# A transformer tower on one core: the keys' bias times the queries, taken from eight more columns of the queries' product

## What is computed

```python
# token reduction: each 4x4 patch (16 pixels) becomes one token of 64 channels, 256 tokens an image
q  = LN(mean over patch) @ Wq.T;  k, v = LN(pixels) @ Wkv.T          # 8 heads of 8
h  = mean + (softmax(q*scale . k over the 16 pixels) . v) @ proj_w.T + proj_b
# causal linear attention with decay over the 256 tokens of an image, chunks of 128
h  = layernorm(h + lightning_attn(h @ w_qkv) @ w_proj + b_proj)
# mixture of experts: 8 experts of 64x64, the best two per token
h  = layernorm(h + moe(h))
```

## Time and profile before

| | |
|---|---|
| Time, median of 3 | 2586.48 us (2584.95 to 2589.83) |
| The profiled execution's own time | 2589.41 us |
| Its span | 2587.0 us |
| PE, DVE, ACT, POOL busy | 87%, 79%, 72%, 71% |
| Mean granted clock of TensorE | 0.985 |

### The profile page before, as it was taken

The page is one execution under the profiler, slowest core; times in us unless marked ns, Lnnn a source line. Parts: engine busy times, 40 slices in busy tenths (PEclk is TensorE's granted clock), DMA queues, the critical chain, the costliest instruction groups (busy, mean ns, idle before and its releaser), DMA issues. The chain is left out here.

```text
span 2587.0 us, 91002 instructions
## 1 busy us (share of the span) xinstructions
PE 2248.5 (87%) x32685; PEld 1057.8 (41%) x32685; DVE 2053.0 (79%) x3996; ACT 1851.1 (72%) x4405; POOL 1839.2 (71%) x1949
## 2 busy tenths in 40 slices
PE   1888898888888888888888888888888885999997
PEld 1344444444444444444444444444444442222222
DVE  4588888887888888888888888888888886777775
ACT  2877777777777777777777777777777773555554
POOL 3688788887888888888888888888888862233333
PEclk9999999999999999999999999999999996999999
DMA  4433333333333333333333333333333300010001
GB/s 79 83 67 67 66 66 66 67 66 57 64 67 67 67 67 67 67 67 67 67 67 67 67 67 67 67 67 67 67 67 67 67 2 1 17 23 22 20 20 29
DMA packets 573783, 147.92 MB, mean 57 GB/s; under 512 B 573504, under 2 KB 573504, under 8 KB 573504
## 3 DMA queue, kind: packets, MB, share of 16 engines
q1 hardware_dynamic: 573504, 143.53, 29.0%
HBM read 135.10 MB, written 8.39 MB: 55 GB/s over the span
## 5 line engine op out<-in xcount | busy, mean ns | idle before, releaser
L709 POOL TENSOR_TENSOR pv<-vs,aw 128x512 f32<-128x512 f32 x512 | 540.2, 1086 | 306.5 <-DVE aw L912 306.5
L856 DVE TENSOR_TENSOR kqs<-ps,qqT 128x512 f32<-128x512 f32 x512 | 354.1, 692 | 299.5 <-PE ps L393 295.2
L595 ACT ACTIVATE xd<-xb 128x512 f32<-128x512 f32 x512 | 585.4, 1178 | 0.0
L388 PE MATMUL ps<-xb,w_ckv 64*64 64x512 f32 x2048 | 555.6, 619 | 5.0 <-DVE kqs L856 5.0
L393 PE MATMUL ps<-xb,w_ckv 64*64 64x512 f32 x2048 | 555.6, 619 | 0.0
L577 ACT ACTIVATE sqs<-ps 128x512 f32<-128x512 f32 x512 | 308.4, 602 | 247.2 <-PE ps L393 246.9
L753 POOL TENSOR_TENSOR xt<-xb 128x512 f32<-128x512 f32 x256 | 325.8, 1273 | 23.0 <-issue 22.6
L716 POOL TENSOR_TENSOR pv<-pv 128x512 f32<-128x512 f32 x256 | 320.5, 1271 | 0.0
L867 DVE TENSOR_TENSOR sm<-ps,decay 128x1024 f32<-128x1024 f32 x256 | 299.5, 1208 | 4.4 <-PE ps L471 4.4
L415 PE MATMUL ps<-w_ckv,xd 64*64 64x64 f32 x16384 | 301.1, 223 | 0.0
L415 PEld LDWEIGHTS ps<-w_ckv,xd 64*64 64x64 f32 x16384 | 266.1, 136 | 33.1 <-issue 3.0
(11 more groups left out here) (223 smaller groups left out, 4261.6 us busy)
## 6 DMA issues: line engine op xcount, KB each, us to landing
xb<-in_x_dram SPq DMA_DIRECT2D x512, 256.0 KB, 4.4
out_dram<-outb SPq DMA_DIRECT2D x128, 64.0 KB, 1.6
w1p<-in_L_ffn_w_dram SPq DMA_DIRECT2D x16, 16.0 KB
w2p<-in_L_ffn_w_dram SPq DMA_DIRECT2D x8, 16.0 KB
b1p<-in_L_ffn_b_dram SPq DMA_DIRECT2D x8, 0.2 KB
b2v<-in_L_ffn_b_dram SPq DMA_DIRECT2D x8, 2.0 KB
sm<-in_L_tok_Wkv_dram SPq DMA_DIRECT2D x4, 16.0 KB, 2.0
w_av<-in_L_attn_w_qkv_dram SPq DMA_DIRECT2D x4, 16.0 KB, 2.1
```

What stands on the lines that cost most here:

```text
L388: nc.tensor.matmul(KB[own, :], w_ckv[own, 2 * P + m * C:2 * P + (m + 1) * C], xv[own, j], start=True, stop=True)
L595: nc.scalar.activation(xd[:, j, :].rearrange("p (b t) -> p b t", b=ST), xb[:, f, :].rearrange("p (b t d) -> p d b t", b=ST, d=ST)[:, j], A ...
L709: nc.gpsimd.tensor_tensor(pv[:, at].rearrange("p (k d) -> p k d", d=D), vs[:, s, at].rearrange("p (k d) -> p k d", d=D), aw[:, j * W4:(j + ...
L856: V.tensor_tensor(kqs[:, j, :].rearrange("p (t d) -> p t d", d=ST), KB.rearrange("p (t d) -> p t d", d=ST), qqT[:, s, :].unsqueeze(2).to_b ...
```

## The change

The bias matmul L369 goes, and the last transpose signals tr_pe. w_qc gets eight more columns, the queries' weights times the keys' bias by head, so L430 writes 136 columns per image. Two DVE instructions behind L891 multiply the eight columns with the root and add cb_row, the keys' bias times the queries' bias, into sbq, a buffer of four slots in SBUF; the softmax reads it two steps later. mx and mxb move from SBUF to columns 25 and 26 in PSUM. The setup gets two small matmuls and four DVE instructions.

```diff
--- before.py
+++ after.py
@@ -111,7 +111,8 @@
         selk = sb("selk", [P, TG])
         selv = sb("selv", [P, TG])
         selbk = sb("selbk", [P, SL])
-        w_qc = sb("w_qc", [P, P])
+        w_qc = sb("w_qc", [P, P + HEADS])
+        cb_row = sb("cb_row", [P, SL])
         w_pj = sb("w_pj", [P, P])
         w_aq = sb("w_aq", [P, P])
         w_av = sb("w_av", [P, 2 * C + CR])
@@ -169,10 +170,9 @@
             y0s = sb1("y0s", [P, N, 3])
             yrs = sb1("yrs", [P, N, 3])
             eps_c = sb1("eps_c", [P, 1])
-            mxb = sb1("mxb", [P, SL])
             sb2 = sb1("sb2", [P, SL])
             aw = sb1("aw", [P, N * SL])
-            mx = sb1("mx", [P, SL])
+            sbq = sb1("sbq", [P, 4, SL])
             den = sb1("den", [P, SL])
             rden = sb1("rden", [P, SL])
             agg = sb1("agg", [P, P])
@@ -329,6 +329,8 @@
                 pe.wait_ge(s_dve0, 1)
                 for j in range(4):
                     nc.tensor.transpose(ps[:, 0, j * P:(j + 1) * P], cat[:, j, :], ident[:])
+                nc.tensor.matmul(ps[:, 5, 0:SL], cat[:, 0, :], selbk[:], start=True, stop=True)
+                nc.tensor.matmul(ps[:, 5, SL:2 * SL], scr[:, 0, :], selbk[:], start=True, stop=True)
                 for j in range(2):
                     nc.tensor.transpose(ps[:, 2, j * P:(j + 1) * P], kqs[:, 0, j * P:(j + 1) * P], ident[:])
                 pe.wait_ge(s_act0, 1)
@@ -365,9 +367,8 @@
                             pe.wait_ge(den_done, done(i, r, 2, 1))
                             sv = ssb[:].rearrange("p (t d) -> p d t", d=ST)
                             for d in range(ST):
-                                nc.tensor.transpose(SB[:, d * P:(d + 1) * P], sv[:, d, :], ident[:])
-                            nc.tensor.matmul(sgr[:, :, 25:26], qqT[:, o, :], selbk[:], start=True,
-                                             stop=True).then_inc(tr_pe, 1)
+                                mm = nc.tensor.transpose(SB[:, d * P:(d + 1) * P], sv[:, d, :], ident[:])
+                            mm.then_inc(tr_pe, 1)
 
                     def keys_free(j):
 
@@ -427,7 +428,7 @@
                                 pe.wait_ge(st_ev, pairs(i, r, 0, 2))
                             for m in range(2):
                                 own = slice(m * C, (m + 1) * C)
-                                mm = nc.tensor.matmul(B67[:, m, 0:P], h1[own, 4 * i + r + 1, 0:P], w_qc[own, :],
+                                mm = nc.tensor.matmul(B67[:, m, 0:P + HEADS], h1[own, 4 * i + r + 1, 0:P], w_qc[own, :],
                                                       start=True, stop=True)
                             mm.then_inc(qp_pe, 1)
 
@@ -805,6 +806,7 @@
                     for m in range(2):
                         link(V.tensor_copy(cat[:, j, m * C:(m + 1) * C], rows[:, j, :]))
                 link(V.tensor_copy(bq_c[:], col[:, 0:1]))
+                link(V.tensor_copy(scr[:, 0, :], col[:, 0:1].to_broadcast([P, P])))
                 link(V.tensor_scalar(selbk[:], headmask[:], col[:, 1:2], WS, ALU.mult, ALU.mult))
                 link(V.scalar_tensor_tensor(w_ckv[:, 0:P], blockmask[:], -1.0 / C, ident[:], ALU.mult, ALU.add))
                 for m in range(2):
@@ -824,8 +826,11 @@
                 for m in range(2):
                     h = slice(m * C, (m + 1) * C)
                     link(V.tensor_scalar(w_qc[h, 0:C], ps[h, 0, m * C:(m + 1) * C], 1.0 / N, None, ALU.mult))
+                    link(V.tensor_scalar(w_qc[h, P:P + HEADS], ps[h, 5, m * HEADS:(m + 1) * HEADS], 1.0 / N, None,
+                                         ALU.mult))
                 for j, dst in ((1, w_ckv[:, 2 * P:3 * P]), (2, w_ckv[:, P:2 * P]), (3, w_pj[:])):
                     link(V.tensor_tensor(dst, ps[:, 0, j * P:(j + 1) * P], blockmask[:], ALU.mult))
+                link(V.tensor_copy(cb_row[:], ps[:, 5, SL:2 * SL]))
                 link(V.tensor_scalar(w_ckv[:, P:3 * P], w_ckv[:, P:3 * P], WS, None, ALU.mult))
                 link(V.tensor_copy(qdec[:], ps[:, 1, 2 * P:3 * P]))
                 link(V.tensor_copy(kqs[:, 1, 0:2 * P], ps[:, 2, 0:2 * P]))
@@ -889,19 +894,25 @@
                     if there(i, r, -1):
                         dve.wait_ge(tq_pe, done(i, r, 0, 1))
                         V.tensor_tensor(heads(q2[:]), B67[:, :, 0:C], yrs[:, 2:4, 2:3].to_broadcast([P, 2, C]),
-                                        ALU.mult).then_inc(q2_done, 1)
+                                        ALU.mult)
+                        for m in range(2):
+                            ins = V.scalar_tensor_tensor(sbq[:, (r + 1) % 4, m * HEADS:(m + 1) * HEADS],
+                                                         B67[:, m, P:P + HEADS], yrs[:, 2 + m, 2:3],
+                                                         cb_row[:, m * HEADS:(m + 1) * HEADS], ALU.mult, ALU.add)
+                        ins.then_inc(q2_done, 1)
                     keys(2)
                     link, n = chain(dve, soft_ch, done(i, r, 2, 5))
                     rs_b = yrs[:, :, 0:2].unsqueeze(3).to_broadcast([P, N, 2, HEADS])
                     sn = sgr[:, :, 0:SL]
+                    mx, mxb = [sgr[:, :, c:c + 1].rearrange("p n w -> p (n w)") for c in (25, 26)]
                     s4 = sn.rearrange("p n (m h) -> p n m h", h=HEADS)
                     if there(i, r, 1):
 
                         link(V.tensor_tensor(s4, s4, rs_b, ALU.mult))
-                        link(V.tensor_reduce(mx[:], sn.rearrange("p n j -> p j n"), AX, ALU.max))
-                        sbias = sgr[:, :, 25:26].rearrange("p n w -> p (n w)")
-                        link(V.tensor_tensor(mxb[:], sbias, mx[:], ALU.add))
-                        link(V.tensor_tensor(sb2[:], sbias, mxb[:], ALU.subtract))
+                        link(V.tensor_reduce(mx, sn.rearrange("p n j -> p j n"), AX, ALU.max))
+                        sbias = sbq[:, (r - 1) % 4, :]
+                        link(V.tensor_tensor(mxb, sbias, mx, ALU.add))
+                        link(V.tensor_tensor(sb2[:], sbias, mxb, ALU.subtract))
                         V.tensor_tensor(sn, sn, sb2[:].unsqueeze(1).to_broadcast([P, N, SL]),
                                         ALU.add).then_inc(s3_done, 1)
                     keys(3)
```

## The result

The changed kernel takes 2591.33 us (median of 20, 2585.54 to 2598.19) against 2586.78 (median of 20): +4.6 us, a ratio of 1.0022 with a 95% interval of 1.0014 to 1.0029. It is slower by a hair, inside the range of 2583.5 to 2599.0, and 2.3 us over the forecast. The interval is clear of 1 but straddles the 0.2% inside which the prediction called a difference none (it gave that 0.62, and slower 0.28). The profiled execution is the slowest of the 20, 2598.19 us, so its span can't be held against the median as a whole. Three executions of the kernel before, of 2681 us and more, were in a slower state of the chip and are left out everywhere.

The account below looks back on a forecast made before the run. The prediction took a loop of TensorE's section and then VectorE's to bound the kernel. Columns 1.6 us plus setup 0.9 us, all else zero, made 2.5 us and a forecast of 2589.0 us, range 2583.5 to 2599.

Parts of the forecast that it names:

- What bounds the kernel: First stage: TensorE's section, then VectorE's, in series; L369 lies beside VectorE's, so removing it gains zero.
- Rival 3: TensorE is the bound after all; 0.29 us a unit come back, 37 us faster, 2552 us; chance 3%.
- The columns: TensorE's query matmuls L430, eight columns wider: 0.012 us a unit on the path, 1.6 us in all.
- The products: Two new VectorE instructions behind L891, 0.225 us each: q2_done 0.29 us later, zero cost, 0.14 us in hand.
- the 0.06 us "for the signal": Between L891's end and L506: 0.49 us, less some 0.06 for the signal, leaves 0.43 for a later q2_done.
- Rival 2: q2_done becomes TensorE's wait in every second unit, from 0.43 us later on: 7.0 us slower, 2596.0 us; chance 9%.
- The setup: Ahead of the first unit: four more VectorE instructions cost 0.9 us; two small matmuls fit into a TensorE wait.
- The sum: Columns 1.6 us plus setup 0.9 us: 2.5 us in all, giving 2589.0 us.
- the likeliest case: The forecast's own case, 2589.0 us, with a range of its own of 2584.5 to 2592.5 us; chance 66%.
- Rival 1: TensorE's clock falls more often at the loop head: five more falls 2596 us, one every iteration 2621; chance 16%.
- Rival 4: Fewer clock falls as their places shift; with none left 10 us come back, 2579 us; chance 6%.
- four signs of being wrong: L506 waiting for VectorE; products over 0.35 us; L856 to L867 not 4.96 us; clock falling at nearly every loop head.

Follow-up runs that it names:

- e1: The kernel before with the bias matmul L369 taken out and nothing added: 2588.52 us, ratio 1.0005.
- e12: The kernel before without the keys' bias, with VectorE's first-stage program written out for all units and an idle-time matmul in TensorE's wait: 2549.28 us.
- e2: The kernel before with eight columns of zeros added to the query matmuls and one memset in the setup, bias matmul kept: 2586.96 us, ratio 1.0000.
- e7: The changed kernel with two more products of the same form, into a buffer nobody reads, ahead of q2_done: 2625.73 us, ratio 1.0149.
- e4: The changed kernel with one matmul whose result nobody reads, put in TensorE's wait for the mask in each unit: 2583.61 us.
- e8: The kernel before, bias matmul in place, with one matmul whose result nobody reads behind it in each unit: 2580.93 us.

## Why the prediction was right, and where it was off

**What bounds the kernel** held. TensorE's distance from the transposes to L457 stayed at 2.04 us with L369 gone, e1 gained nothing from leaving it out, and e12 nothing from two instructions in VectorE's idle stretch. Rival 3 (TensorE is the bound, 37 us) fell with e1. The size of the wait was off, 1.56 us forecast and 1.40 measured (2.6 and 2.44 at the loop head), because L369's two records overlap the transposes and leave 0.13 us, not 0.29.

**The columns**: 1.6 us forecast, 128 x 0.011 = 1.4 measured in e2 and the changed kernel.

**The products**: 0.225 us each forecast, 0.216 measured; q2_done 0.29 us later forecast, 0.27 measured; free of GpSimd, as L924 had promised: 214 to 222 ns in all 256 cases. What failed is the 0.06 us "for the signal": L507 starts 0.25 us behind the products, in the changed kernel and in e7, while in the first unit of the changed kernel L440 follows the products by 0.06. So not 0.14 us was in hand but nothing, and q2_done became the last wait in every second unit by 0.03 us, Rival 2 at its threshold. It cost nothing because the matmul behind L507 starts 0.03 us closer to it. That the products came out free is therefore partly luck: the forecast's 0.14 us of room wasn't there. e7 shows the price just beyond. Why the transpose into bank 6 needs 0.25 us isn't settled.

**The setup**: 0.9 forecast; the first query matmul moved from 52.59 to 53.39, 0.8 us. Missed was the first unit, where nothing hides the products. TensorE's timeline of the changed kernel and then of the kernel before:

```profile
53.39 0.83 PE L431 MATMUL ps<-w_qc,h 64*128 64x136 f32 x4 [0.85 <-DVE w_av L845]
57.50 0.47 PE L440 MATMUL ps<-ident,q 128*128 128x128 f32 x1 [3.28 <-DVE sbq L899]
```

```profile
52.59 0.80 PE L430 MATMUL ps<-w_qc,h 64*128 64x128 f32 x4 [0.85 <-DVE w_av L840]
56.40 0.48 PE L439 MATMUL ps<-ident,q 128*128 128x128 f32 x1 [3.01 <-DVE q L891]
```

4.11 us from the one matmul to the other in place of 3.81: 0.3 us. Missed as well was the fall at 91 us, some 0.8 us in the pair e4 and e8; the forecast looked for falls at the loop head alone.

**The sum** of the path is then 1.4 + 0.8 + 0.3 = 2.5 us, as forecast, though by other terms; with the fall at 91 us it is 3.3, against 2.8 ± 0.8 between e4 and e8. **What was left out of the likeliest case** is the clock: 2.5 to 2.8 us more of falls, Rival 1 in its mildest form. I had set "little work to lose" against it and put the forecast's own case at no change; two more falls of 1.4 us each (2.8), about what was measured, stood only in the range. 2.5 + 2.5 is 5.0 of the 5.3 between the means. Rival 4 (fewer falls) didn't come, and its price, 10 us for all of them, was too high: the extra matmul brought the kernel before 5.7, after some 1.0 us of its own cost in the first units (first L458 of e8 at 99.67 us, first L456 at 98.64).

Of the four signs of being wrong none came. L507 shows no wait, though it is late by 0.03 us; the products take 0.22 us; L872 starts 4.96 us behind L861 as before; the clock is low in 8 stretches of 29.

The Trainium skill, TensorE: Matmul & The Clock Gate, section "HAM oscillation — how this bites in real kernels", describes another kernel, in which a wait for DMA in every iteration, longer than the waits here, makes each next start cold. The traces agree that a recurring wait can do this, but not that each does: with waits of 2.2 to 2.5 us the clock was low in 2 to 8 stretches of 29, and in 22 with e7's timing.

## What to carry to other kernels

Before taking work off an engine, look whether the instruction behind it waits: where it does, the work was free, and taking it out can cost clock (here 2.8 ± 0.8 us). Price a dependency from the last instruction that signals it, with the delay measured at that receiver and not at another one, and do the first, uncovered unit of a pipeline by itself. A wait that is 1 us longer in one unit out of four is worth more than all the small edits: here the loop's head held 36 us, some 6 of them falls.

## What the runs showed that I had not expected

A matmul whose result nobody reads, about 0.9 us in TensorE's wait for the mask in every unit, made both kernels faster: 5.7 and 8.2 us. And the length of a wait doesn't settle how often the clock falls: 24 of e7's 34 us were falls, at a loop-head wait 0.2 us shorter than the changed kernel's. Whether its iteration, 0.18 us longer, is the cause, these runs don't show.
